# A residual and a column of node numbers, added to a tile by one accumulating transfer of GpSimd (second attention layer)

## The reference, cut to what matters

```python
h = _gat_conv(x, W1, att_src1, att_dst1, b1, src, dst)
h = jax.nn.elu(h)
h = _gat_conv(h, W2, att_src2, att_dst2, b2, src, dst)
h = jax.nn.elu(h)                      # _L1_gnn_ref returns this
...
x = _layernorm(x + _L1_gnn_ref(x, edge_index, ...), axis=-1)
```

## Time and profile before

| | us |
|---|---|
| median of 3 executions | 6393.06 |
| lowest and highest | 6388.5 and 6402.69 |
| the profiled execution | 6399.0 |
| its span, first to last instruction | 6397.3 |
| the layer `l2` in it, about | 3150 to 3880 |

### The profile page before, as it was taken

How to read it: one execution, slowest core, us unless ns; L and a number is a source line. 1 busy time by engine, 2 the same in 40 slices (tenths; PEclk the granted TensorE clock), 3 DMA queues, 4 the chain that set the end, 5 groups by cost and what they waited for, 6 DMA issues and landing times. The chain is left out here.

```text
span 6397.3 us, 74087 instructions
## 1 busy us (share of the span) xinstructions
PE 4260.0 (67%) x18797; PEld 3091.6 (48%) x18797; DVE 4604.8 (72%) x15011; ACT 3125.1 (49%) x6788; POOL 3809.3 (60%) x3139
## 2 busy tenths in 40 slices
PE   2488882058885988588866678997898477880000
PEld 1177772047774877477512224556777355560000
DVE  5645554644444876699599996968887899957776
ACT  0033331023332665588555556766776377772333
POOL 5767775767774777565255525721111688747776
PEclk9599996579997999799877778998999688895555
DMA  8944446954443997899698888989997678756665
GB/s 315 371 78 79 79 74 193 378 159 80 80 80 78 321 311 280 270 316 316 213 305 295 304 266 327 399 306 324 341 347 287 225 278 292 274 199 233 237 239 196
DMA packets 616389, 1558.26 MB, mean 244 GB/s; under 512 B 126988, under 2 KB 283090, under 8 KB 599038
## 3 DMA queue, kind: packets, MB, share of 16 engines
q1 hardware_dynamic: 430270, 1159.75, 51.8%
q0 software_dynamic: 185696, 393.77, 22.3%
HBM read 794.19 MB, written 811.66 MB: 251 GB/s over the span
## 5 line engine op out<-in xcount | busy, mean ns | idle before, releaser
L864 POOL DMA_INDIRECT NS<-e_tot,e_idx x392 | 633.5, 1616 | 241.5 <-ACT e_tot L1118 92.5
L1802 POOL DMA_INDIRECT l_eg<-HBT,k_nsrc x392 | 481.4, 1228 | 351.9 <-POOLq L161 120.6
L989 DVE TENSOR_SCALAR e_eq<-e_pk,z_skey 128x128 f32<-128x128 f32 x588 | 186.9, 345 | 627.6 <-DMA NS<-e_tot,e_idx 598.1
L2408 PE MATMUL l_pm<-k_w_L3b,l_zt 128*128 128x258 f32 x1568 | 414.2, 424 | 118.5 <-ACT l_o L2467 117.8
L1255 POOL DMA_INDIRECT XH<-n_o,z_home x392 | 384.2, 980 | 165.6 <-issue 113.1
L2382 PE MATMUL l_ps<-l_a,k_ident 128*128 128x512 f32 x392 | 309.0, 881 | 222.9 <-DVE l_a L2660 211.6
L2546 ACT ACTIVATE l_a<-l_a,l_eshare 128x64 f32<-128x64 f32 (+1 forms) x980 | 280.5, 373 | 308.8 <-DVE l_eshare L2064 308.8
L2408 PE MATMUL l_pm<-k_w_L1b,l_zt 128*128 128x264 f32 x1568 | 384.0, 400 | 51.1 <-ACT l_o L2467 50.8
L2022 DVE SCALAR_TENSOR_TENSOR l_erun<-l_erun,k_same,l_eg 128x260 f32<-128x260 f32 (+2 forms) x880 | 414.9, 471 | 3.3 <-issue 0.2
L2408 PEld LDWEIGHTS l_pm<-k_w_L3b,l_zt 128*128 128x128 f32 x1568 | 328.5, 215 | 180.6 <-issue 126.9
L2737 DVE BATCH_NORM_STATS2 l_bs<-l_a 128x6 f32<-128x256 f32 x1016 | 402.1, 413 | 1.3
(11 more groups left out here) (442 smaller groups left out, 13304.1 us busy)
## 6 DMA issues: line engine op xcount, KB each, us to landing
HBT<-l_o SPq DMA_DIRECT2D x196, 528.0 KB, 4.3
l_a<-HBT SPq DMA_DIRECT2D x156, 528.0 KB, 6.0
GSUMS<-l_erun SPq DMA_DIRECT2D x72, 1056.0 KB, 5.9
NS<-z_zero SPq DMA_DIRECT2D x100, 520.0 KB, 9.1
l_a<-XH SPq DMA_DIRECT2D x98, 528.0 KB, 6.0
HA<-n_o SPq DMA_DIRECT2D x98, 528.0 KB, 4.6
l_a<-HA SPq DMA_DIRECT2D x98, 528.0 KB, 6.8
X<-l_z SPq DMA_DIRECT2D x98, 520.0 KB, 7.7
```

The costliest lines, as they stand in the source:

```text
L864: pool.indirect_dma_start(out=nodes, out_offset=bass.IndirectOffsetOnAxis(ap=idx[q % DEEP][:, k:k + 1], axis=0), in_=tot[q % 2][:, k, :], ...
L1802: pool.indirect_dma_start(out=self.g[b % self.ng][:, k, :], out_offset=None, in_=self.table, in_offset=bass.IndirectOffsetOnAxis(ap=self.i ...
L2408: last = pe.matmul(self.pm[h][:, i, 0:self.wc], zt[:, k, h * (J // 2) + i, :], self.weight[:, k, 0:self.wc], start=k == 0, stop=k == KC - 1)
```

## The change

The buffers `r`, their loads on SP and the two DVE operations are gone for this layer. Instead:

- A new stage `add` (tick body + 1 = 9): POOL waits for the ELU of the tile and for a zeroed column, and issues one transfer with `accum_op=ALU.add`, which adds the 257 columns of `x1` to columns 0 to 256 of the tile `a` in SBUF.
- So that the node number arrives unspoilt in column 256, ACT writes zeros there, ahead of the exp (`s_zc`). In the stage norm, ACT copies the column to `S["ids"]`.
- A new stage `stat` (tick body + 2 = 10) holds the four row statistics, at whose head DVE waits for the transfer. The stages var and norm come two ticks later (11 and 15), the store at 16, and `a` has 14 buffers.

```diff
+        if kind == "l1b":
+            L["add"], L["stat"] = body + 1, body + 2
         if self.norm:
-            L["var"], L["norm"] = body + 1, body + 5
+            L["var"], L["norm"] = L.get("stat", body) + 1, L.get("stat", body) + 5
...
-        if now and self.resid is not None:
+        if now and self.resid is not None and not self.summed:
...
                 pool.tensor_tensor(self.rs[b][:], self.ve[b][:], S["minus_half"][:, 0:2 * J], ALU.pow).then_inc(self.s_rs, 1)
+        now = self.tile(tick, "add") if self.summed else None
+        if now:
+            u, region, t = now
+            pool.wait_ge(self.s_zc, u + 1)
+            pool.wait_ge(self.s_elu, u + 1)
+            pool.dma_start(self.a[u % self.ra][:, :, 0:D + 1], tile_rows(self.resid, region, t), accum_op=ALU.add).then_inc(self.s_added[u % 3], 16)
...
                 col = region * C + J * t
+                act.activation(S["ids"][:, col:col + J], a[:, :, D], ACT.Copy)
                 act.activation(z[:, :, D], S["dinv"][:, col:col + J], ACT.Copy)
...
+                if self.summed:
+                    act.wait_ge(self.s_in[u % self.ra], self.loaded(u))
+                    act.activation(a[:, :, D], S["dinv"][:, 0:J], ACT.Copy, scale=0.0).then_inc(self.s_zc, 1)
...
+        now = self.tile(tick, "stat") if self.summed else None
+        if now:
+            parts.append(self.summed_stats(dve, now[0]))
...
             elu.then_inc(self.s_elu, 1)
-            yield
-            dve.wait_ge(self.s_elu, u + 1)
-            r = self.r[u % self.rr]
-            dve.wait_ge(self.s_rin[u % self.rr], 16 * (u // self.rr + 1))
-            dve.tensor_copy(S["ids"][:, col:col + J], r[:, :, D])
-            dve.tensor_tensor(a[:, :, 0:D], a[:, :, 0:D], r[:, :, 0:D], ALU.add).then_inc(self.s_u, 1)
+            return
...
+    def summed_stats(self, dve, u):
+        dve.wait_ge(self.s_added[u % 3], 16 * (u // 3 + 1))
+        yield from self.row_stats(dve, u)
```

More of the change, by code:

```diff
@@ L2168, in __init__ @@
         self.s_in = s.sems("rows_loaded", self.ra)
-        if resid is not None:
+        if kind == "l1b":
+            self.s_added = [s.pool_sem(S, f"residual_added{b}") for b in range(3)]
+            self.s_zc = s.sem("id_column_zeroed")
+            self.s_id = s.sem("node_ids_kept")
+        elif resid is not None:
             self.rr = 4
```

## The result

| | before | after |
|---|---|---|
| median, us (4 runs each) | 6391.22 | 6522.35 |
| lowest and highest | 6388.5 and 6402.69 | 6519.19 and 6525.43 |
| span of the profiled execution | 6397.3 | 6523.7 |
| layer `l2`, its first load to the next layer's first load | 730 | 869 |

The ratio is 1.0202, with a 95% interval of 1.0184 to 1.0219. Forecast were 6472 us and a range of 6320 to 6605: the direction holds and so does the mechanism in the main, but the size is 52 us too small at 79 against 131.

A forecast was written before the change was run, and what follows sets the result against it. DVE was taken to set the pace (busy 681 of the layer's 730 us), DMA engines close behind. Middle 37 + tail 23 + front 11 + end 8 = +79 us on 6393 gave 6472 us, range 6320 to 6605.

The forecast's parts named there:

- The loop: DVE's `stat`, `ve`, POOL's power, transfer, next `stat` but one: 16.0 us a middle pair against 15.1, +37 us.
- T: Issue to landing of the accumulating transfer: 8.8 us, from 7.2 plain load plus 1.6 second read; bounds 5.7 and 12.4.
- The hand-over: From the end of `ve` through the power to POOL's next issue: 2.0 us.
- The head: On DVE, from a tick's first operation to the end of `ve`: 4.1 and 6.4 us, say 5.2, less the removed 1.4.
- The assumption on odd tiles: Odd tiles have nearly two ticks between ELU and `stat`; only even tiles have the power in between.
- The ends: Layer's short-tick ends lose more: tail +23 us, front +11, one more transfer at the very end +8.
- The removed work: DVE loses the add (1.213 us) and copy (0.179) per tile, 1.39 together, 136.5 us for 98 tiles.
- The other two resources: DMA engines need 6.9 to 8.1 us a tick with the second read; POOL 6.1 to 9.2, lower half taken.
- Faster (1): Transfer costs the old load's price, T is 5.7, DMA engines give 399 GB/s: -77 us, 6316; chance 0.23.
- POOL as the bound (2): Descriptors for 512 rows cost 4.2 us, POOL needs 9.2 us in ticks with gathers: about +220, 6613; chance 0.12.
- A transfer dearer than two reads (3): On the DMA engines, three times the load's bytes, 9.7 us a tick: +210, so 6600; chance 0.10.
- Even (4): T near 7.2, gains in the layer's middle pay for its ends: 6393 us; chance 0.10.

The follow-up runs named there:

- both remedies: Changed kernel with row statistics one tick later and the accumulating transfer issued at the head of POOL's tick, ahead of gathers and power: 6387.48 us, ratio 0.9986.

## Why the prediction was right in kind and short in size

**The loop.** It was named with its place and its terms, and the runs with slack and with the transfer moved confirm it. The terms over the 40 pairs of the middle, as means of the start times in the trace of after, from one even tile's statistics to the next even tile's:

| | forecast | all 40 | the 19 in which DVE waits for the even tile | the other 21 |
|---|---|---|---|---|
| head of `stat` to the end of `ve` | 5.2 | 5.8 | 6.2 | 5.3 |
| `ve` to the next issue | 2.0 | 2.8 | 2.9 | 2.8 |
| issue to the statistics, T | 8.8 | 8.8 | 9.0 | 8.7 |
| pair | 16.0 | 17.4 | 18.1 | 16.8 |

The three add up to the pair by construction, so the sum alone proves no loop: it closes only in the 19 in which DVE waits for the even tile. In 15 of the other 21 it is the odd tile that DVE waited for on the way. T, which no row of before showed, came out as taken, and this is partly luck. It was meant as the landing, and the even tiles' landings have a mean of 8.0 us and a median of 6.9; only where DVE waits for them are they 9.0. In the other 21 pairs the 8.7 us hold 1.8 us in which the transfer had already landed. The two terms with rows were too short. The hand-over was read from one instance, in which nothing but `ve` held the power; it is 1.7 us at least and 5.3 at most, and in the turn shown above `z` or the gathers stood in the way. The head was averaged from two instances, and the removed 1.4 us was too much, see below. Both misses are small, but a pair was forecast at only 0.9 us above before, so 1.4 us more makes it 2.3: over 41 pairs 94 us instead of 37. The mis-sized terms are these two, head and hand-over.

**The assumption on odd tiles** was wrong. They were to have nearly two ticks; by the same start times they were issued 3.5 us after the ELU in the median, and 8.3 at most. DVE waits for odd tiles as well (39 waits between 3204 and 3917, 19 of them for the even tile of a pair and 20 for the odd one). Their transfers take 10.9 us to land on average, where T was 8.8 for all. The step that failed is the sentence that gave odd tiles nearly two ticks and named only the power as what is in front of the transfer. In the turn on POOL shown above the gathers, gated by DVE, stand there too. Moved ahead of the power alone, the transfer gave 26 us; moved ahead of both, 120.

**The ends.** Tail +23 forecast, 15 measured; front +11, 15; drain +8, 13. In the tail the ticks were 52 / 9 = 5.8 us instead of the 6.7 of a pair of 13.4; why wasn't looked into. The drain counted one transfer, and not that stages var to store come two ticks later as well; I take the 5 us for that, which is not shown; one tick more made the drain only 1.2 us longer (35.1 against 33.9).

**The removed work** falls away: DVE is busy 567.41 us of the longer stretch (3150 to 4000) where it was 681.23. The gain was given back entirely by the wait of 240.6 us. But the removal was priced too high: from tile 8 to tile 89 DVE is busy for 584.23 us before and 498.39 after, 1.06 us less a tile, where 1.39 was forecast.

**The other two resources.** The second read costs 1.3 to 1.9 us of the DMA engines a tick, forecast was 1.6. That they "may bound just as late as the loop" is half right: they bound at 7.2 us a tick (62 ELUs in 446), not at 8.0, and only once the loop is gone. The issue on POOL costs 1.43 us against bounds of 1.06 and 4.2: the lower half was right.

**The rivals.** Faster (1): no. Its turning point, "where T is under about 7 us", was wrong too. With T = 6.4 the plain transfer is still 35 us slower than before, since head and hand-over take 8.6 us together and leave 15.1 - 8.6 = 6.5 for it in the middle, with nothing for the ends. POOL as the bound (2): no, it is busy 384.25 of 714 us in the middle. A transfer dearer than two reads (3): no, by the same 1.3 to 1.9 us. Even (4): only with slack or with another place in the queue.

**The signs named ahead.** A wait of over 200 us in front of the statistics: 240.6. Landing 8 to 10: 9.2 in the median of all, 6.9 and 11.0 by even and odd tiles. POOL 1 to 2 us: 1.43. ELUs 8 us apart: 8.7; 6 to 7 in the tail: 5.8. A DMA share of 0.95 or more: 0.94. DVE idle in about every second tick: 39 waits in 82 ticks, though not the even ones alone.

## What to carry to other kernels

When a load made ahead of time is replaced by a transfer that can only start once the result is there, count the ticks between the two as you would count a buffer: issue, landing and all that stands ahead of the issue on its in-order queue must fit, here 9 to 12 us of landing and 3.5 to 6.5 us of queue into two ticks of 7.6, of which the ELU takes 1.2. Before the change is judged, give it one more stage of slack and put the issue at the head of its engine's tick; here that is 135 us apart from the kernel as written. And then ask what the freed engine will run into: the accumulating transfer takes 1.06 us of DVE off a tile and puts 1.3 to 1.9 us on the DMA engines, which were 0.87 busy already.

## What the runs showed of the hardware

- An accumulating transfer of 514 KB in 512 rows of 1028 bytes from HBM into SBUF lands after 5.8 us at the quickest, a plain one from the same queue, in fewer packets, after 3.8. On POOL its issue takes 1.43 us, the plain one's 0.81.
- The landing is longer in the kernels with a higher DMA share: 9.2 us in the median at 0.94 (after), 11.5 and 11.9 at 1.10 (with slack, and with both remedies). But the mean share doesn't fix it: at 0.92 and 0.95 it is 6.6 us for even tiles alone and 10.1 for odd tiles alone. What is under way at the issue goes with it (1.1 gathers at the even tiles', 1.9 at the odd tiles' in after); that this is the cause isn't shown.
- Only GpSimd can issue it, by the Trainium skill ("DMA: Bandwidth & Descriptors", SWDGE vs HWDGE vs iDMA), so another engine's queue was no way out; no run here tried one.
- A small DVE operation costs less than its record says when the next one doesn't wait. In the kernel before, the copy takes 0.16 us by its record and the addition behind it starts 0.07 us later; the addition of 1.21 us is followed after 1.14:

```profile
3518.98 0.16 DVE L2669 COPY k_ids<-l_r 128x4 f32<-128x4 f32 x1
3519.05 1.21 DVE L2670 TENSOR_TENSOR l_a<-l_a,l_r 128x1024 f32<-128x1024 f32 x1
3520.19 0.18 DVE L2750 TENSOR_TENSOR l_mv<-l_bs 128x8 f32<-128x8 f32 x1
```

By these start times the two removed operations held DVE for 1.21 us, where the forecast had 1.39. Over 81 tiles DVE's busy time fell by 1.06 us each.
